# Last two layers of a gated cross-attention stack: order of scatters, of the last chunk's routing and of the first queries

## The chip, the cores and the metric

The kernel runs on one core of one Trainium2 chip. Times are microseconds on the device for one execution of the whole program, the median of several runs. The engines are TensorE (PE; its weight loads are PEld), VectorE (DVE), ScalarE (ACT), GpSimd (POOL) and SyncE (SP, which here only issues DMAs). They run side by side, each through its own list of instructions in order, and wait for each other by semaphores.

## What is computed

Four layers act on x, 2 batches of 1024 tokens of 256 features in float32. Each layer is

```
x = x + tanh(g_xattn[L]) * cross_attention_L(layernorm(x), context of 154 rows of 192)
x = x + tanh(g_ffn[L])   * ffn_L(layernorm(x))
```

The change concerns layers 2 and 3. Their attentions have 16 heads of 16. That of layer 3 normalises each whole query and each whole key to unit length, adds the unnormalised query to its output (the residual), and ends in a layer norm of its own:

```
Qp = query @ Wq + bq;  Q = l2norm(Qp);  K = l2norm(key @ Wk + bk);  V = value @ Wv + bv
out = softmax(Q K^T * SCALE) V
y = out @ Wo + bo + Qp
return (y - mean(y)) / sqrt(var(y) + 1e-5) * ln_gamma + ln_beta
```

The ffn of layer 2 is a mixture of 8 experts of width 512, each token to its top two with softmax gates, plus biases b2 by gate. That of layer 3 is a mixture of 16 experts of width 352 (top two, 320 places for each expert) plus one shared expert for all tokens.

## The kernel before

The tokens lie in 16 tiles of 128, and 4 tiles make a chunk c of 512. Phase 4 is the attention of layer 2, phase 5 its experts, phase 6 the attention of layer 3, phase 7 its experts. X holds the residual stream in SBUF, Y the normalised tokens.

The order of work in an attention of 16 heads is one list of steps, made by steps16(L) (lines 545 to 633). Every engine walks through the same list and does its own part of each step, so that a step's place in the list is its place in the queue of each engine that has a part in it, and an engine can start a step only when it is through with its parts of all steps ahead. A chunk has four groups g of four heads. The steps of a group are: "scores" (scores of the first 128 keys, four PE matmuls of 32 rows, L820, and the exponentials on ACT, L1280), "rem" (the same for the remaining 26 keys of four heads at once, L838), "av" (probabilities times values, L849 and L852, copied by ACT, L1325) and, two groups later, "norm" (transposes L861, division by the sums on DVE, L1949 and L1952). "turn back" (L868) and "tail" follow once for a chunk: tail multiplies by Wo (output, L726), and DVE adds the result, L1737 in layer 2, L1966 in layer 3.

PSUM is used as two rings of four banks, RP and RQ. An engine that takes a bank waits until the reader of the bank's previous use is through.

Preparing a chunk takes these steps in layer 3: "combine" (DVE adds the two results of layer 2's experts to X, L2359, once they have come back from DRAM), "stats" (DVE statistics L1713 and L1716, then POOL's inversion, rsqrt, L1599 and L1601), "normal" (DVE, L1722), "yT" (PE transposes L667, ACT copies L1249), "proj" (PE L779; DVE adds bq, L1921, into Y; ACT sums the squares, L1303; POOL inverts the length), "unit" (DVE scales to unit length, L1930; then POOL adds bo to Y, the residual, L1653) and "turn" (PE transposes L788, ACT copies L1313). Before the change, chunks 0 and 1 are prepared ahead of the first scores, and chunk c + 2 between the groups of chunk c (lines 592 to 599).

Behind its tail a chunk of layer 3 has "post": DVE's statistics in tail (L1969, L1972), POOL's inversion (L1661), DVE's normalisation L1977, times gamma L1982, added to X L1984. The bias ln_beta and the like is added to all of X once, by POOL (add_row, L1578), and the first use waits for it (xbias). Steps that begin with "next" belong to the routing for the experts: next stats, next normal (L1722), next yT, "next lg" (router logits, PE L1092, DVE L2381, in layer 3 softmax), "next top" (the two best of each token, one-hots, gates; in layer 2 it needs one exponential of ACT, L1415, and signals oh_made in the middle), "next pos" (PE counts places by matmuls L1100 and L1102, DVE makes slot indices in slots, L2275 to L2291; for the last chunk of layer 2 also the table of which expert each tile has, tile_table), "next scatter" (POOL issues 8 indirect DMAs for a chunk, one for each tile and choice, L1626, which write the token rows to their slots in DRAM), and in layer 2 "next G" and "next b2" (gates by expert: DVE gates_by_expert L2298 and L2300, PE transposes L1110, ACT copy L1418, PE L1118, DVE L2398). The order of POOL's work matters to the change: in it stand the inversions, the additions of bo, add_row and the scatters.

Steps that begin with "ahead" prepare keys and values of layer 3 while layer 2 still runs: "ahead keys turned" transposes the normalised keys (PE L741 and L742); DVE spreads them into even and odd heads (spread_keys, L1871), and POOL copies the last 26 keys (L1642). "ahead values" are matmuls L697 and L698 and DVE's additions (values, L1764 and L1787).

Behind the attention of layer 2 the tiled experts start: SP loads the first three W1 once tile_table is made, and the token tiles once all 32 scatters of the layer have landed (lines 2557 to 2562); PE transposes them (L1158) and multiplies (L1167, L1176). In layer 3, SP waits for all scatters likewise, and PE starts with L1190 and L1133.

The order that the diff replaces at the end of layer 2 and at the start of layer 3:

```
return o + [("av", z, 3), ("norm", z, 2), ("next yT", z - 1), ("norm", z, 3), ("next lg", z - 1),
            ("turn back", z), ("next top", z - 1), ("tail", z), ("next stats", z), ("ahead values", 0, 0),
            ("next pos", z - 1), ("next normal", z), ("next scatter", z - 1), ("next G", z - 1), ("next yT", z),
            ("ahead keys turned", 0), ("next lg", z), ("next top", z), ("ahead values", 0, 1), ("next pos", z),
            ("next scatter", z), ("next b2", z - 1), ("next G", z), ("next b2", z)]
...
o = [("combine", 0), ("stats", 0), ("combine", 1), ("normal", 0), ("yT", 0), ("stats", 1), ("proj", 0),
     ("normal", 1), ("yT", 1), ("combine", 2), ("unit", 0), ("proj", 1), ("turn", 0), ("stats", 2),
     ("unit", 1), ("turn", 1)]
```

## Time and profile before

| what | value |
|---|---|
| median of 3 runs | 1545.22 us (1532.24, 1545.22, 1550.62) |
| the profiled execution | 1543.91 us, span in the trace 1542.1 us |
| mean granted TensorE clock | 0.904 of full speed |
| busy PE, PEld, DVE, ACT, POOL | 1314.2, 812.8, 711.5, 474.8, 301.6 us |
| last matmuls ahead of the layer-2 experts, first of theirs | until 902.6 us, from 908.2 us |
| first scores of layer 3 | 1104.4 us |
| first tokens of layer 3's routed experts on PE | 1306.9 us |

All trace times count from the start of the span. Busy times overlap, since the engines run side by side; what is worth time is where PE idles or is slowed, and what it waited for there. The granted clock is 0.50 or 1.00 at any moment, so a mean between them says how much of a stretch ran at half.

### The profile page before, as it was taken

To read this page: it belongs to the slowest core of one execution; us is meant where nothing else is said; L and a number is where in the kernel's file an instruction comes from. 1 tells how busy PE (TensorE), PEld (TensorE's weight loads), DVE (VectorE), ACT (ScalarE), POOL (GpSimd) and SP (SyncE) were. 2 spreads that over 40 slices of the span, in tenths; PEclk is the share of its full clock that TensorE was granted. 3 is DMA by queue.
4 is the path that set the end of the run, shared out by engine and by line. 5 is a ranking of instruction groups with operands and counts; after the bars stand their busy time and mean duration, and the time that the engine had idled before them with its cause. 6 is when DMAs were issued, how large, how long until landed. Compare 5 with 4: busy or idle time off the path is not lost.

```text
span 1542.1 us, 18540 instructions
## 1 busy us (share of the span) xinstructions
PE 1314.2 (85%) x6487; PEld 812.8 (53%) x6513; DVE 711.5 (46%) x2010; ACT 474.8 (31%) x890; POOL 301.6 (20%) x373
## 2 busy tenths in 40 slices
PE   5999979959999856499989869994789877999997
PEld 2645444334565542354544559994544444666664
DVE  5755353386323458876563532223436464122214
ACT  1144434411222216304434113331364321222220
POOL 5200010023000010424022322222242215122220
PEclk9699989969999887769999669997799779999999
DMA  9990010010000010010000456665000022344425
GB/s 263 285 279 1 1 52 0 0 59 0 1 0 1 0 32 0 1 19 1 1 29 28 148 167 211 214 208 184 2 1 22 21 71 95 121 160 151 136 82 172
DMA packets 106201, 124.12 MB, mean 80 GB/s; under 512 B 15138, under 2 KB 90654, under 8 KB 106110
## 3 DMA queue, kind: packets, MB, share of 16 engines
q1 hardware_dynamic: 99118, 104.05, 22.9%
q0 software_dynamic: 6992, 18.88, 3.3%
q8 instruction: 54, 0.88, 0.2%
q14 instruction: 37, 0.30, 0.1%
HBM read 74.05 MB, written 48.86 MB: 80 GB/s over the span
## 4 chain that ended last, share of the span: by engine, by line
PE 74%; DVE 12%; issue 5%; POOL 4%; ACT 3%; DMA 1%; SPq 1%; DVEq 0%; POOLq 0%; ACTq 0%
PE bank L1133 9%; PE bank L726 5%; PE bank L1167 5%; PE bank L1209 4%; PE bank L1176 4%; PE bank L800 4%; PE bank L709 4%; PE bank L820 4%; PE bank L991 3%; PE bank L838 3%; PE bank L849 3%; PE bank L852 2%; PE bank L667 2%; PE bank L901 2%; POOL x_slots L1626 2%
## 5 line engine op out<-in xcount | busy, mean ns | idle before, releaser
L1280 ACT ACTIVATE scratch<-bank 128x512 f32<-128x512 f32 x240 | 126.4, 603 | 96.1 <-PE bank L827 44.2
L1133 PE MATMUL bank<-scratch 128*128 128x320 f32 (+3 forms) x480 | 154.0, 478 | 0.6 <-issue 0.6
L1599 POOL TENSOR_SCALAR rstd<-mv 128x4 f32<-128x4 f32 x36 | 10.2, 284 | 669.0 <-DVE mv L1716 644.4
L1936 DVE TENSOR_REDUCE scratch<-bank 128x2 f32<-128x308 f32 x256 | 105.7, 472 | 72.0 <-PE bank L800 69.7
L1133 PEld LDWEIGHTS bank<-scratch 128*128 128x128 f32 (+1 forms) x480 | 87.1, 185 | 61.3 <-issue 30.2
L2437 DVE TENSOR_TENSOR scratch<-scratch,bank 128x320 f32<-128x320 f32 (+3 forms) x60 | 31.4, 526 | 177.9 <-PE bank L1133 174.6
L1249 ACT ACTIVATE scratch<-bank 128x512 f32<-128x512 f32 x56 | 32.0, 599 | 222.4 <-PE bank L667 222.2
L1626 POOL DMA_INDIRECT x_slots<-scratch x64 | 66.7, 1042 | 106.3 <-DVEq L2294 88.5
L667 PE MATMUL bank<-ident,scratch 128*128 128x128 f32 x224 | 41.9, 349 | 52.9 <-DVE scratch L1722 34.5
L726 PE MATMUL bank<-weights,scratch 128*128 128x256 f32 x320 | 79.9, 409 | 6.2 <-ACT scratch L1344 2.7
L820 PE MATMUL bank<-scratch 32*128 32x512 f32 x384 | 82.2, 649 | 2.3 <-ACT scratch L1325 1.8
L800 PE MATMUL bank<-scratch 32*128 32x308 f32 x512 | 81.7, 525 | 1.3 <-DVEq L1795 1.3
L1167 PEld LDWEIGHTS bank<-scratch 128*128 128x128 f32 x624 | 77.5, 196 | 2.7 <-issue 0.8
L1167 PE MATMUL bank<-scratch 128*128 128x128 f32 x624 | 77.9, 279 | 0.4 <-issue 0.4
L1700 POOL DMA_INDIRECT y_back<-scratch x48 | 45.1, 940 | 158.2 <-ACT scratch L1474 138.9
L726 PEld LDWEIGHTS bank<-weights,scratch 128*128 128x128 f32 x320 | 64.4, 206 | 21.8 <-ACT scratch L1344 3.9
L1176 PE MATMUL bank<-scratch 128*128 x312 | 73.9, 380 | 1.3 <-ACT scratch L1430 1.3
L2420 DVE TENSOR_TENSOR scratch<-bank,weights 128x512 f32<-128x512 f32 x39 | 27.0, 692 | 103.5 <-PE bank L1167 103.5
L709 PE MATMUL bank<-scratch,weights 128*128 128x512 f32 x128 | 67.4, 680 | 5.6 <-ACT scratch L1249 5.6
L800 PEld LDWEIGHTS bank<-scratch 32*128 32x128 f32 x512 | 51.6, 207 | 34.5 <-DVE scratch L1936 11.4
L1209 PE MATMUL bank<-scratch 128*128 128x256 f32 (+3 forms) x288 | 68.9, 387 | 0.6 <-DVE scratch L2437 0.6
L667 PEld LDWEIGHTS bank<-ident,scratch 128*128 128x128 f32 x224 | 34.5, 182 | 63.7 <-issue 36.6
(372 smaller groups left out, 2300.1 us busy)
## 6 DMA issues: line engine op xcount, KB each, us to landing
scratch<-in_L_ffn_W SPq DMA_DIRECT2D x47, 512.0 KB
x_slots<-zeros SPq DMA_DIRECT2D x1, 17680.0 KB, 72.1
scratch<-y_back SPq DMA_DIRECT2D x16, 512.0 KB, 8.0
scratch<-in_L_ffn_w_gate SPq DMA_DIRECT2D x16, 352.0 KB
scratch<-in_L_ffn_w_up SPq DMA_DIRECT2D x16, 352.0 KB
x_slots<-zeros SPq DMA_DIRECT2D x1, 5200.0 KB, 89.0
scratch<-x_slots SPq DMA_DIRECT2D x39, 130.0 KB, 3.1
y_back<-zeros SPq DMA_DIRECT2D x1, 4352.0 KB, 38.7
```

Source lines behind the costliest of these rows:

```text
L667: last = pe.transpose(bk[:, i * P:(i + 1) * P], v["Y"][:, TPC * c + i, d * P:(d + 1) * P], ident[:])
L709: last = pe.matmul(bk[:], v["Wq"][:, k, m * P:(m + 1) * P], v["yT"][:, k, :], start=k == 0, stop=k == DK - 1)
L726: last = pe.matmul(bk[:, i * D:(i + 1) * D], o[:, tt * P:(tt + 1) * P], v["Wo"][:, m, :], start=m == 0, stop=m == len(rows) - 1)
L800: pe.matmul(bk[:, 0:2 * M], v["QT"][rows, c, m, t * P:(t + 1) * P], v["Kz"][rows, m, b, :, :].rearrange("p e k -> p (e k)"), start=True, s ...
L820: last = pe.matmul(bks[r][:], v["Kz"][rows, m, b, e, 0:P], v["QT"][rows, c, m, :], start=True, stop=not has_max)
L1133: last = pe.matmul(bk[0:fn, 0:n], w[s][:, k, m * P:m * P + fn], moving(k), start=k == 0, stop=k == DK - 1)
L1167: last = pe.matmul(bk[:, m * P:(m + 1) * P], v["W1"][:, i % 3, k, m * P:(m + 1) * P], v["xeT"][:, i % 2, k * P:(k + 1) * P], start=k == 0, ...
L1176: last = pe.matmul(bk[:, 0:D], v["hT"][:, i % 2, m, :], v["W2"][:, bass.ds(expert[i] * (H2 // P * D) + m * D, D)], start=m == 0, stop=m == ...
L1209: last = pe.matmul(bk[0:n, i % 2 * D:(i % 2 + 1) * D], v["hT"][0:fn, e % 2 * 3 + m, i * P:i * P + n], v["Wd"][s][0:fn, m, :], start=m == 0 ...
L1280: act.activation(v["PT"][:, n % 2, j, :], bk[:], ACT.Exp, scale=float(v["hd"]) ** -0.5).then_inc(RP.read, 1)
L1626: pool.indirect_dma_start(x2_slots if L == 2 else x3_slots, bass.IndirectOffsetOnAxis(ap=q["sidx"][:, n:n + 1], axis=0), q["Yx"][:, t, :], ...
L1936: dve.tensor_reduce(v["mx"][:, TPC * c + t, r, 2 * m:2 * m + 2], bk[:, 0:2 * M].rearrange("p (e k) -> p e k", k=M), AX.X, ALU.max)\
```

## The change

Six edits, all in the order of steps or in who does a step:

1. In both layers, "next scatter" of chunks 0 and 1 moves from group 2 to the end of group 3 of the chunk, behind the inversions of "post" and "next stats" in POOL's queue.
2. At the end of layer 2, "next pos" and "next scatter" of chunk 2, then the normalisation, come ahead of both "ahead values"; the last chunk's "next yT" and "next lg" come ahead of "ahead keys turned" and of "next G". DVE's part of G becomes a step of its own ("next gates"), ahead of the last logits for chunk 2.
3. The keys are turned through ring RP, and ACT instead of DVE spreads them; POOL's copy of the last 26 keys is a step of its own behind the last scatter.
4. Layer 3 prepares only chunk 0 ahead of the first scores. Chunks 1 to 3 are prepared between the groups of chunks 0 and 1, by two tables (first: ahead of "rem"; second: behind "av"); chunk 3's "turn" falls into chunk 2, group 0. Its combines and statistics move along.
5. POOL adds the bias row to X at chunk 1, group 1 instead of chunk 0, group 3.
6. In layer 3 the wait for that row stands in "post" of chunk 0 instead of in its tail.

```diff
             else:
-                o = [("combine", 0), ("stats", 0), ("combine", 1), ("normal", 0), ("yT", 0), ("stats", 1), ("proj", 0),
-                     ("normal", 1), ("yT", 1), ("combine", 2), ("unit", 0), ("proj", 1), ("turn", 0), ("stats", 2),
-                     ("unit", 1), ("turn", 1)]
+                o = [("combine", 0), ("stats", 0), ("normal", 0), ("yT", 0), ("combine", 1), ("proj", 0), ("stats", 1),
+                     ("unit", 0), ("normal", 1), ("turn", 0)]
+
+                first = {(0, 0): [("yT", 1), ("combine", 2)], (0, 1): [("combine", 3)], (0, 2): [("stats", 3)],
+                     (0, 3): [("normal", 3)]}
+                second = {(0, 0): [("proj", 1), ("stats", 2)], (0, 1): [("unit", 1), ("normal", 2)], (0, 2): [("turn", 1), ("yT", 2)],
+                      (0, 3): [("proj", 2)], (1, 0): [("unit", 2), ("yT", 3)], (1, 1): [("turn", 2)], (1, 2): [("proj", 3)],
+                      (1, 3): [("unit", 3)], (2, 0): [("turn", 3)]}
...
-                ahead = c + 2 < NC
+                ahead = L < 3 and c + 2 < NC
...
-                    if L == 3 and c == 0:
-                        o += {0: [("normal", 2)], 1: [("combine", 3)], 2: [], 3: []}[g]
+                    if L == 3:
+                        o += first.get((c, g), [])
...
-                            o += {0: [("next yT", c - 2)], 1: [("next lg", c - 2)], 2: [("next pos", c - 2), ("next scatter", c - 2)],
+                            o += {0: [("next yT", c - 2)], 1: [("next lg", c - 2)], 2: [("next pos", c - 2)],
                                   3: [("next b2", c - 2)]}[g]
                     if L == 3 and c > 1:
-                        o += {0: [("next normal", c - 2)], 1: [("next lg", c - 2)], 2: [("next pos", c - 2), ("next scatter", c - 2)],
+                        o += {0: [("next normal", c - 2)], 1: [("next lg", c - 2)], 2: [("next pos", c - 2)],
                               3: []}[g]
...
                         o.append(("av", *divmod(n - 1, 4)))
+                    if L == 3:
+                        o += second.get((c, g), [])
...
-                    if L == 3 and c == 0:
-                        o += {0: [], 1: [("stats", 3)], 2: [("normal", 3)], 3: []}[g]
...
-                            o += {0: [], 1: [("next top", c - 2)], 2: [("next G", c - 2)], 3: []}[g]
+                            o += {0: [], 1: [("next top", c - 2)], 2: [("next gates", c - 2), ("next G", c - 2)], 3: [("next scatter", c - 2)]}[g]
                     if L == 3:
                         if c and g == 3:
                             o += [("post", c - 1), ("next stats", c - 1)]
                         if c > 1:
-                            o += {0: [("next yT", c - 2)], 1: [("next top", c - 2)], 2: [("next res", c - 2)], 3: []}[g]
+                            o += {0: [("next yT", c - 2)], 1: [("next top", c - 2)], 2: [("next res", c - 2)], 3: [("next scatter", c - 2)]}[g]
...
-                            ("turn back", z), ("next top", z - 1), ("tail", z), ("next stats", z), ("ahead values", 0, 0),
-                            ("next pos", z - 1), ("next normal", z), ("next scatter", z - 1), ("next G", z - 1), ("next yT", z),
-                            ("ahead keys turned", 0), ("next lg", z), ("next top", z), ("ahead values", 0, 1), ("next pos", z),
-                            ("next scatter", z), ("next b2", z - 1), ("next G", z), ("next b2", z)]
+                            ("turn back", z), ("next top", z - 1), ("tail", z), ("next stats", z), ("next pos", z - 1),
+                            ("next scatter", z - 1), ("next normal", z), ("ahead values", 0, 0), ("ahead values", 0, 1),
+                            ("next yT", z), ("next gates", z - 1), ("next lg", z), ("ahead keys turned", 0), ("next G", z - 1),
+                            ("next top", z), ("next pos", z), ("next scatter", z), ("ahead last keys", 0), ("next b2", z - 1),
+                            ("next gates", z), ("next G", z), ("next b2", z)]
...
-                        bk = RQ.take(pe, p, "k", m)
+                        bk = RP.take(pe, p, "k", m)
...
+                    if what == "ahead keys turned":
+
+                        for m in range(MT):
+                            bk = RP.get(act, 6, "k", m)
+                            a = bk[:, 0:B * M].rearrange("p (b k) -> p b k", k=M)
+                            for e in range(2):
+                                st.did(act.activation(ph[6]["Kz"][:, m, :, e, :], a, ACT.Copy, scale=odd[:, e:e + 1]))
+                            st.wait()
+                            act.sem_inc(RP.read, 1)
+                            act.sem_inc(kz16_made, 1)
...
-                    elif what == "scores" and L and (c, i[0]) == (0, 3 if L == 3 else 0):
+                    elif what == "scores" and L and (c, i[0]) == ((1, 1) if L == 3 else (0, 0)):
                         add_row((v["gb"] if L == 3 else v["gbo"])[:], gbo_made, L, p)
...
-                        if L and c == 0:
+                        if L in (1, 2) and c == 0:
                             dve.wait_ge(xbias, XB[p])
...
                     elif what == "post":
+                        if c == 0:
+                            dve.wait_ge(xbias, XB[p])
                         dve.wait_ge(post_z, c + 1)
```

## Rows read from the trace of the kernel before

**Rows 1.** Windows by stage: busy time of each engine, then PEclk, DMA share, GB/s

```profile
core 0: us, PE busy (x) PEld busy (x) DVE busy (x) ACT busy (x) POOL busy (x), PEclk, DMA share, GB/s
910.00:1059.00 149.00, 147.46 (x1010) 138.96 (x1010) 40.00 (x145) 52.85 (x115) 36.28 (x38) 0.98 0.64 194
1059.00:1309.00 250.00, 189.66 (x934) 106.61 (x933) 124.23 (x415) 86.48 (x176) 78.13 (x73) 0.85 0.16 52
```

**Rows 2.** Timeline of PE, end of layer 2: start, us, line, op, [idle before <- releaser]

```profile
874.72 1.01 PE L1110 MATMUL bank<-ident,scratch 128*8 128x128 f32 x4 [4.85 <-DVE scratch L2300]
...
879.74 3.58 PE L1092 MATMUL bank<-weights,scratch 128*128 128x8 f32 x16
...
910.28 2.05 PE L1167 MATMUL bank<-scratch 128*128 128x128 f32 x8 [0.38 <-issue]
```

**Rows 3.** Timelines of DVE and, in the last row, of POOL there

```profile
884.52 0.19 DVE L2381 TENSOR_TENSOR scratch<-bank,weights 128x32 f32<-128x32 f32 x1 [3.69 <-PE bank L1092]
...
888.69 0.42 DVE L1764 TENSOR_TENSOR scratch<-bank,weights 128x256 f32<-128x256 f32 x1
...
891.25 0.17 DVE L2291 CAST scratch<-scratch 128x8 uint32<-128x8 f32 x1
...
900.66 0.96 POOL L1626 DMA_INDIRECT x_slots<-scratch  x1 [0.30 <-issue]
```

**Rows 4.** Timeline of PE, start of the last attention

```profile
1077.43 1.94 PE L667 MATMUL bank<-ident,scratch 128*128 128x128 f32 x8 [18.22 <-issue]
1080.06 6.28 PE L779 MATMUL bank<-weights,scratch 128*128 128x256 f32 x16 [0.69 <-ACT scratch L1249]
...
1090.86 6.00 PE L779 MATMUL bank<-weights,scratch 128*128 128x256 f32 x16 [0.69 <-ACT scratch L1249]
...
1102.51 1.97 PE L788 MATMUL bank<-ident,scratch 128*128 128x128 f32 x8 [4.78 <-DVE scratch L1930]
1104.41 2.15 PE L820 MATMUL bank<-scratch 32*128 32x512 f32 x8
...
1107.89 1.04 PE L667 MATMUL bank<-ident,scratch 128*128 128x128 f32 x8
...
1113.77 3.72 PE L779 MATMUL bank<-weights,scratch 128*128 128x256 f32 x16
```

**Rows 5.** Timelines of POOL, then of DVE, in the last attention

```profile
1073.80 1.99 POOL L1601 TENSOR_TENSOR rstd<-rstd,nhalf 128x4 f32<-128x4 f32 x1
...
1079.45 1.04 POOL L1601 TENSOR_TENSOR rstd<-rstd,nhalf 128x4 f32<-128x4 f32 x1
...
1103.06 2.35 POOL L1653 TENSOR_TENSOR scratch<-scratch,weights 128x1024 f32<-128x1024 f32 x1 [0.18 <-POOL rstd L1601]
...
1101.32 1.14 DVE L1930 TENSOR_SCALAR scratch<-scratch 128x256 f32<-128x256 f32 x4 [2.00 <-POOLq L1649]
1102.97 3.56 DVE L1722 TENSOR_SCALAR scratch<-X,mv,rstd 128x256 f32<-128x256 f32 x4 [0.51 <-POOLq L1570]
...
1273.24 1.37 DVE L1722 TENSOR_SCALAR scratch<-X,mv,rstd 128x256 f32<-128x256 f32 x4
```

**Rows 6.** Timeline of PE behind the projection of chunk 2

```profile
1121.20 1.13 PE L838 MATMUL bank<-scratch 128*128 128x512 f32 x2 [2.06 <-ACT scratch L1280]
```

**Rows 7.** DVE's post step in chunk 1; waits 1062:1310 (total, times, longest); PE's transposes

```profile
1162.75 1.38 DVE L1977 TENSOR_SCALAR scratch<-scratch,mv,rstd 128x256 f32<-128x256 f32 x4 [0.93 <-POOLq L1661]
...
DVE scratch L1977 <- POOLq L1661: 8.1, 3, 4.2
...
1171.53 1.09 PE L667 MATMUL bank<-ident,scratch 128*128 128x128 f32 x8 [1.93 <-DVE scratch L1722]
...
1206.98 1.97 PE L667 MATMUL bank<-ident,scratch 128*128 128x128 f32 x8 [6.45 <-DVE scratch L1722]
...
1247.80 1.97 PE L667 MATMUL bank<-ident,scratch 128*128 128x128 f32 x8 [7.38 <-DVE scratch L1722]
```

**Rows 8.** Windows from a chunk's y transposes to the end of the next output

```profile
1171.50:1189.60 18.10, 18.07 (x119) 10.50 (x119) 8.22 (x47) 8.73 (x17) 3.02 (x3) 1.00 0.04 16
1207.00:1231.70 24.70, 24.51 (x120) 13.90 (x120) 8.20 (x46) 8.95 (x17) 3.27 (x4) 0.70 0.03 12
```

8 lines of the change are left out of this document (3 added, 5 removed).

## The prediction

> **What bounds the kernel now.** I read the busy times by stage first. The stretch from 1059 to 1309 us, the last attention with the shared half of the last experts, is the loosest: TensorE (PE) is busy 189.7 of 250 us and its mean granted clock is 0.85 [rows 1]. The same view of 910 to 1059, the layer-2 experts, has PE busy 147.5 of 149, so nothing can be won there; the change touches only what lies around it. Next comes PE's own order of instructions, and in it each row that begins with idle time: those are the places where another engine is last. Last come the waits of DVE and POOL, to see which link of the chain ended each gap. PE is the bound while it is fed. It is starved at the end of layer 2, where the last scatter of tokens is late [rows 2, 3], at the start of the last attention [rows 4], and before the transposes of a normalised chunk [rows 7]. A starved place can cost twice: the idle time, and the work behind it at half clock.
>
> **Part 1: end of layer 2.** Now PE waits 4.85 us for DVE ahead of G (L1110), because DVE does values(0) and the slots ahead of the normalisation; then come the transposes of y, the turned keys and, from 879.7, the last chunk's logits (16 matmuls, 3.58 us at half clock) [rows 2]. DVE's own chain from these logits to slot indices runs from 884.5 to 891.4, 6.9 us, of which values(1), from 888.69 to the slots at about 890.5, are 1.8 with their hand-overs [rows 3]. The eighth scatter is issued until 901.6, and the first tile's matmuls start 8.7 us after that (910.28) [rows 2, 3].
> The new order: values(0) (1.8) leave DVE's queue ahead of the normalisation, so the transposes of y can start at about 873.1 (G's place less 1.6). PE does both values meanwhile: 16 matmuls of 256 columns, like the 3.72 us of the projection at full clock [rows 4]. Then at full clock 1.0 of transposes, 1.2 for the copies of ScalarE (ACT), 1.9 of logits: they are in DVE at 877.3 instead of 884.5. DVE's chain is now 5.3 (6.9 less values, plus hand-over), and up to 0.9 more, because ACT now spreads the keys, four activations, ahead of the one exponential that DVE waits for in the middle. Indices at 883.5, hand-over 0.2, eight issues of 0.96 with 0.30 between [rows 3] end at 893.7: 7.9 us earlier, and 8.9 if the exponential isn't late. At half clock the logits take 3.58 and the turned keys behind them some 2.5, the exponential is 2.2 us late for DVE, and the same sum gives 3.2. I take 5.5, the middle: PE no longer idles at 870, but it does only short work there, and the clock was half behind such work. The POOL copy of the last keys goes behind the scatter and is first read in the next attention, 150 us of experts away [rows 1]. The scatters of chunks 0 and 1 of this layer move behind one inversion of 1.3 us: nothing. The first expert weights are requested right behind the table of tiles, which moves forward too. **-5.5** (-3.2 to -8.9).
>
> **Part 2: start of the last attention.** DVE's second combine leaves the side of POOL's first inversion, whose power step took 1.99 instead of 1.04 us [rows 5], and the normalisation no longer stands behind it: the first transposes come 1.9 us earlier, at 1075.5 [rows 4]. From there PE does the transposes of y(0) (1.94), waits 0.7 for copies, projects (6.28, half clock); then comes the chain of bias, squares, inversion, scaling. For chunk 1 that chain is seen: projection's end 1096.86, turn at 1102.51, 5.65 us [rows 4]. So the turn of chunk 0 begins at 1090.2, takes 2.0 and 0.7 for the copy, and scores(0,0) start at 1093.0 instead of 1104.4: -11.4. What left the front is done between the groups: transposes 1.04, projection 3.72, turn another 1.04 at full clock [rows 4], +5.8. A projection between groups also holds the exponentials on ACT behind its squares; PE waited 2.06 us for that behind the projection of chunk 2 [rows 6], and chunk 3's does the same. In the new order chunks 1 and 2 have it, while chunk 3's projection is followed by the output matmuls, which cover it: two stalls against two; I add 0.75, because the first falls where nothing else is queued. -11.4+5.8+0.75 = **-4.85** by the end of chunk 0's output. Bounds: +1 with the moved work at half clock (it then costs 5.8 more), -8 if the stalls go.
>
> **Part 3: the last queries meet the post-norm.** In chunk 1, group 3, the step "unit 3" now stands right ahead of "post 0". Now DVE is free at 1161.82 and waits 0.93 for POOL's inversion [rows 7]. After: DVE scales the queries (1.14, L1930), only then POOL may add bo to the residual (2.35, L1653), and the inversion (about 0.3 and 1.04) is queued behind that on POOL [rows 5]. With three hand-overs of 0.1 that is 1161.82+1.14+2.35+1.35+0.3 = 1166.96 for the post step's start against 1162.75: **+4.2**. Behind it stand the post step, the statistics, the normalisation, and PE's transposes, which already waited 1.93 [rows 7]; so PE's idle becomes 6.1 us. Behind a gap of 6.45 at the same place one chunk later the stretch up to the next output took 24.7 us at mean clock 0.70, against 18.1 at 1.00 behind the gap of 1.93 [rows 7, 8]. The 120 and 119 matmuls are the same work, so I charge **+6.5** for it here; the lower bound is 0, if the clock holds. The bias row that POOL adds to X moves to chunk 1, group 1, where POOL has nothing due for two groups, and its wait moves to the post step: nothing; if POOL were held by it past the inversion, the price would be this part's again.
>
> **Part 4: scatters at a chunk's end.** In chunks 2 and 3 POOL's eight scatters (10.1 us) stand ahead of the post-norm's inversion, and DVE waits: of 8.1 us in three waits 0.9 belong to chunk 1, 4.2 and 3.0 to these [rows 7]. Behind the inversions they hold nobody up; DVE's own residual step and norm take as long as the inversion, so nothing is next: **-4.1** and **-2.9**. PE's gaps shrink from 6.45 to 2.3 and from 7.38 to 4.5 [rows 7]. Gaps of 1.93 and 2.06 had full clock behind them, so the half-clock loss of chunk 2 goes: **-6.5**. A gap of 4.78 had half clock behind it (the turn at 1102.51 took 1.97) [rows 4], so chunk 3 keeps its loss: 0, at best -2.5.
> The scatters now start together with DVE's normalisation, for which PE waits. The one such case in the trace, chunk 3's normalisation at 1273.24 with a scatter issued beside it, took 1.37 for its four instructions [rows 5]: nothing. A POOL tensor operation beside the same four made them 3.56, which is 2.2 more [rows 5]; twice that is the upper end, +4.4.
> The Trainium skill (GPSIMD Engine Reference, section Key points) says that GpSimd shares its SBUF interfaces with VectorE and contends with it in a two-port mode or with two SBUF inputs. By it alone a scatter would count like the tensor operation, and the sum would be 4.4 us higher; the row of the scatter speaks against that.
>
> **Sum.** -5.5-4.85+4.2+6.5-4.1-6.5-2.9 = -13.15. The profiled execution took 1543.91 (span 1542.1 and 1.8 around it): 1530.8. The median of the runs shown is 1.3 above that execution, so 1532. Those three runs lie within 1532 to 1551, and 1% is about what a measurement can tell from no change.
>
> **Rivals.**
> A, the clock holds behind the new gap of part 3: 1532-6.5 = 1525.5. For: the gap is 0.35 shorter than the one that lost it, and dense work (two remainder groups) stands right ahead of it. Against: the gaps of 4.78, 6.45 and 7.38 all had half clock behind them [rows 4, 7]. 0.20.
> B, the clock falls in chunk 2 too, behind the shorter gap: 1538.5. For: the work behind it is the same that did not bring the clock back for over half of 24.7 us [rows 8]. Against: it stayed full behind 1.93 at this very place. 0.15.
> C, the earlier indices gain nothing in layer 2 (the exponential behind the keys, G and b2 still to do, weights late): 1537.5. For: PE has two rounds of G and b2 left behind the slots, some 10 us. Against: the scatter and its landing take 19 from the same point, and none of the others was last before. 0.10.
> D, a scatter beside the normalisation holds it like a POOL tensor operation: 1536.4. Against: the row of 1.37. 0.07.
> E, on the other side: one late post-norm (part 3) puts PE to half clock, and until the last output it does not come back, so that the two shorter gaps find it low. A chunk of 29 us of PE work, stretched like the first stretch here (24.7/18.1) throughout, costs 10.6 instead of 6.5, and so does the next, in place of part 4's gain of 6.5: 1532+4.1+10.6+6.5 = 1553. It decides once the clock stays low for more than the one stretch of 24.7 us. Against: the mean of 0.70 says that it came back within that stretch. 0.04.
> F, the gaps move but are filled by other waits, so that it cancels: about 1545. 0.06.
> The forecast itself, 1527 to 1537: 0.38.
>
> **Numbers.** Faster by over 1% means below 1529.8: A nearly whole, and the forecast's own lower third and more (part 1 at its -8.9, a share of measurement spread): 0.41. Slower by over 1%: E, 0.04. The rest within 1%: 0.55. The range from 1520 (A with part 1's best end and a little more) to 1546 leaves out E and the tails.
>
> **What would show it.** Right: scores(0,0) some 11 us earlier after the first combine; a gap of about 6 us on PE ahead of the y(0) transposes, ended by DVE L1722, with half clock behind it; DVE's waits for the post inversion of about 4, 0 and 0 us; gaps of about 2.3 and 4.5 in chunks 2 and 3; last layer-2 scatter to first tile still 8.7 us. Wrong: the gap in chunk 1 below 3 us (then POOL's order was misread), a normalisation of over 2 us beside a scatter, or a stretch from the layer-2 experts' end to the routed experts that is not about 8 us shorter.

## The result, and the profile of the changed kernel

The changed kernel took 1532.6 us (seven runs, 1528.15 to 1533.95) against 1545.22 (seven runs, 1532.24 to 1550.62): ratio 0.9938, 95% interval 0.9909 to 0.9967. The forecast of 1532 fits, and the direction with it; the time saved is below 1%. Two later series of the same kernel gave 0.9905 (0.9867 to 0.9943) and 0.9978 (0.9951 to 1.0004), so about 9 us is a better figure for the gain than the 12.6 of the first medians. The profiled execution took 1533.95 (span 1532.2).

The windows by stage (the columns are those of [rows 1]). The first row covers the same 250 us of the span as the last row there, so it starts later in the work: it holds the last attention, the shared half of the last experts and some 11 us more of the routed ones. The second row is the layer-2 experts, which now start at 897.4.

```profile
1059.00:1309.00 250.00, 204.28 (x962) 115.14 (x962) 124.04 (x418) 87.94 (x179) 76.37 (x72) 0.82 0.14 48
897.40:1047.50 150.10, 148.21 (x1014) 138.70 (x1014) 39.99 (x145) 53.32 (x116) 36.48 (x38) 0.98 0.63 194
```

PE is busier in the 250 us (204.3 for 189.7 before), but its mean clock is lower, 0.82 for 0.85. The experts of layer 2 are as they were.

The timeline of PE has the places that [rows 2, 4, 7] showed, now with new times and gaps (start, length, line, [idle before <- releaser]; L673 is L667 of before, L794 is L788, L826 is L820, L844 is L838, L1164 is L1158, and DVE's L1738 is L1722):

```profile
869.03 1.09 PE L673 MATMUL bank<-ident,scratch 128*128 128x128 f32 x8 [0.87 <-DVE scratch L1738]
...
897.40 0.66 PE L1164 MATMUL bank<-ident,scratch 128*128 128x128 f32 x2 [5.83 <-issue]
...
1064.11 1.94 PE L673 MATMUL bank<-ident,scratch 128*128 128x128 f32 x8 [16.64 <-issue]
...
1079.02 1.97 PE L794 MATMUL bank<-ident,scratch 128*128 128x128 f32 x8 [5.65 <-DVE scratch L1944]
1081.88 2.09 PE L826 MATMUL bank<-scratch 32*128 32x512 f32 x8 [0.89 <-ACT scratch L1329]
...
1120.51 2.08 PE L844 MATMUL bank<-scratch 128*128 128x512 f32 x2 [2.06 <-ACT scratch L1286]
...
1162.51 1.97 PE L673 MATMUL bank<-ident,scratch 128*128 128x128 f32 x8 [6.01 <-DVE scratch L1738]
...
1199.93 1.97 PE L673 MATMUL bank<-ident,scratch 128*128 128x128 f32 x8 [3.84 <-DVE scratch L1738]
...
1237.44 1.97 PE L673 MATMUL bank<-ident,scratch 128*128 128x128 f32 x8 [6.74 <-DVE scratch L1738]
```

Scores(0,0) start at 1081.88 instead of 1104.41; the first combine came at 1056.76 instead of 1068.18, so 11.1 us of the 22.5 are won behind it. The gap ahead of the y(0) transposes has grown from 1.93 to 6.01 us; those of y(1) and y(2) have shrunk from 6.45 and 7.38 to 3.84 and 6.74.

The reason for the new gap stands in DVE's and POOL's timelines of chunk 1 (L1944 is "unit 3", L1669 POOL's addition of bo, L1615 and L1617 the inversion, L1993 the post step, L1977 in [rows 7]):

```profile
1148.60 1.13 DVE L1944 TENSOR_SCALAR scratch<-scratch 128x256 f32<-128x256 f32 x4
1153.75 1.38 DVE L1993 TENSOR_SCALAR scratch<-scratch,mv,rstd 128x256 f32<-128x256 f32 x4 [4.02 <-POOLq L1677]
...
1161.07 1.38 DVE L1738 TENSOR_SCALAR scratch<-X,mv,rstd 128x256 f32<-128x256 f32 x4 [0.91 <-POOLq L1586]
```

```profile
1149.81 2.35 POOL L1669 TENSOR_TENSOR scratch<-scratch,weights 128x1024 f32<-128x1024 f32 x1 [3.39 <-DVE scratch L1944]
1152.24 0.23 POOL L1615 TENSOR_SCALAR rstd<-mv 128x4 f32<-128x4 f32 x1
1152.56 1.04 POOL L1617 TENSOR_TENSOR rstd<-rstd,nhalf 128x4 f32<-128x4 f32 x1
```

That is part 3 of the prediction, link by link: scaling, addition of bo, inversion, post step. The windows behind the gaps of chunks 1 and 2 answer to [rows 8]:

```profile
1162.50:1186.10 23.60, 23.59 (x119) 13.62 (x119) 8.23 (x47) 8.95 (x17) 0.00 (x0) 0.73 0.00 1
1199.90:1223.60 23.70, 23.67 (x120) 13.69 (x120) 8.21 (x46) 8.95 (x17) 7.34 (x8) 0.73 0.13 46
```

The first ran at 1.00 before and now at 0.73, as forecast. The second should have gone from 0.70 to 1.00 and did not: the gap of 3.84 has half clock behind it, too. That is rival B, in part.

So the time fits, but these two profiles don't show it to come from where the prediction put it. Their spans differ by 9.9 us. Of these, 4.1 lie ahead of the end of layer 2's last output, 6.7 between there and the first expert tile, and 0.6 in the layer-2 experts, while the attention of layer 3, from its first combine to the y(2) transposes, is 1.1 us longer than before (180.7 for 179.6), where the prediction's parts 2 to 4 had 7.65 less; 0.5 more is lost behind it.

### The profile page after: what moved, and what is told of

The parts are those of the page before. It is cut to its first block, busy times and chain, and to the rows that moved or that the text cites. A ratio compares the mean times of both kernels' runs of the same rounds, so it can differ in the third digit from the quotient of the medians.

```text
span 1532.2 us, 18567 instructions
## 1 busy us (share of the span) xinstructions
PE 1315.4 (86%) x6513; PEld 810.8 (53%) x6513; DVE 709.6 (46%) x2006; ACT 477.1 (31%) x894; POOL 300.6 (20%) x373
## 4 chain that ended last, share of the span: by engine, by line
PE 76%; DVE 12%; issue 4%; POOL 3%; ACT 3%; DMA 1%; SPq 1%; DVEq 0%; POOLq 0%; ACTq 0%
PE bank L1139 9%; PE bank L732 5%; PE bank L1173 5%; PE bank L806 4%; PE bank L1215 4%; PE bank L1182 4%; PE bank L715 4%; PE bank L826 4%; PE bank L855 3%; PE bank L844 3%; PE bank L997 3%; PE bank L858 2%; PE bank L673 2%; PE bank L907 2%; PE bank L867 1%
## 5 line engine op out<-in xcount | busy, mean ns | idle before, releaser
L1615 POOL TENSOR_SCALAR rstd<-mv 128x4 f32<-128x4 f32 x36 | 11.2, 311 | 739.1 <-DVE mv L1732 686.1
L673 PE MATMUL bank<-ident,scratch 128*128 128x128 f32 x224 | 42.2, 351 | 51.5 <-DVE scratch L1738 34.1
L826 PE MATMUL bank<-scratch 32*128 32x512 f32 x384 | 83.6, 662 | 1.5 <-ACT scratch L1329 0.9
L1642 POOL DMA_INDIRECT x_slots<-scratch x64 | 65.4, 1022 | 29.8 <-issue 18.1
L673 PEld LDWEIGHTS bank<-ident,scratch 128*128 128x128 f32 x224 | 34.5, 183 | 62.7 <-issue 36.6
```

Source lines behind the costliest of these rows:

```text
L673: last = pe.transpose(bk[:, i * P:(i + 1) * P], v["Y"][:, TPC * c + i, d * P:(d + 1) * P], ident[:])
L826: last = pe.matmul(bks[r][:], v["Kz"][rows, m, b, e, 0:P], v["QT"][rows, c, m, :], start=True, stop=not has_max)
L1642: pool.indirect_dma_start(x2_slots if L == 2 else x3_slots, bass.IndirectOffsetOnAxis(ap=q["sidx"][:, n:n + 1], axis=0), q["Yx"][:, t, :], ...
```

## The experiments

One profile can't separate the terms, because the clock's level differs from execution to execution. So each experiment is read in two ways: by its ratio to the kernel before (measured on the same chip), and by the lengths of the stages of its profile, which repeat to 0.1 us wherever the clock does. The stages, with the starts and ends that bound them:

- R: end of the last output of layer 2 to the first expert tile
- S: first combine to the end of chunk 0's output
- T: from there to the y(0) transposes
- U: from the y(0) transposes to the end of chunk 1's output
- V: to the y(1) transposes; W: to the end of chunk 2's output; Z: to the y(2) transposes

| kernel | ratio | R | S | T | U | V | W | Z |
|---|---|---|---|---|---|---|---|---|
| before | 1 | 40.8 | 90.5 | 12.9 | 18.1 | 17.4 | 24.7 | 16.1 |
| changed | 0.9938 | 34.0 | 88.7 | 17.0 | 23.6 | 13.8 | 23.7 | 13.8 |
| e1 scatters alone | 0.9973 | 40.3 | 91.3 | 12.9 | 22.7 | 13.8 | 23.7 | 13.8 |
| e2 routing alone | 0.9974 | 36.6 | 89.2 | 12.9 | 18.0 | 17.4 | 24.7 | 16.1 |
| e3 queries alone | 0.9992 | 40.4 | 85.5 | 17.0 | 19.3 | 17.4 | 24.6 | 16.1 |
| e4 unit 3 later | 0.9965 | 37.0 | 85.0 | 12.9 | 25.1 | 13.8 | 23.8 | 13.8 |
| e5 changed again | 0.9905 | 34.2 | 85.7 | 17.0 | 19.3 | 13.8 | 22.6 | 13.8 |
| e6 without routing | 0.9938 | 39.8 | 85.0 | 17.0 | 19.3 | 13.8 | 22.6 | 13.8 |
| e7 without queries | 0.9914 | 34.2 | 90.7 | 12.9 | 18.1 | 13.8 | 22.7 | 13.8 |
| e8 without scatters | 0.9955 | 33.2 | 85.2 | 17.0 | 19.2 | 17.4 | 19.7 | 16.1 |
| e9 exponential first | 0.9958 | 34.4 | 89.0 | 17.0 | 23.6 | 13.8 | 23.7 | 13.8 |
| e10 residual earlier | 0.9948 | 37.6 | 88.5 | 17.0 | 23.6 | 12.9 | 22.5 | 12.9 |
| e11 three moves | 0.9929 | 34.8 | 85.6 | 12.9 | 25.1 | 12.9 | 21.0 | 12.9 |
| e12 changed, third | 0.9978 | 36.9 | 84.6 | 17.0 | 19.2 | 13.8 | 22.6 | 13.8 |

e1 to e4 ran on one chip, e5 to e8 on a second, e9 to e12 on a third. Half the width of the intervals is about 0.003, or 4.6 us.

**e1: the scatters alone** (of the kernel before; the lines of layer 3, those of layer 2 are alike)

```diff
-2: [("next pos", c - 2), ("next scatter", c - 2)],
+2: [("next pos", c - 2)],
...
-1: [("next top", c - 2)], 2: [("next res", c - 2)], 3: []}[g]
+1: [("next top", c - 2)], 2: [("next res", c - 2)], 3: [("next scatter", c - 2)]}[g]
```

> The kernel before with part 4 alone: the scatters of chunks 0 and 1 of both layers at the end of group 3. By the prediction's terms: DVE's waits for the post inversion in chunks 2 and 3 fall from 4.2 and 3.0 us to about 0.7 (what the profile of the changed kernel shows there), the gaps ahead of the transposes of y(1) and y(2) from 6.45 and 7.38 to about 2.5 and 4.5, and full clock behind the first of them: -13.5, so 1532. Rival (clock falls behind the shorter gap too, as in the changed kernel's profile): -7, so 1538. Rival (the whole gain of the change is this part, the rest cancels): 1532.6, the changed kernel's own time, with the clock at half in chunk 2. Rival (scatters beside the normalisation hold it): a normalisation of over 2 us in chunks 2 and 3.

Measured: 1542.44 against 1544.48, ratio 0.9973 (0.9943 to 1.0002). V and Z shrink by 3.6 and 2.3 us, and W only by 1.0: half clock behind the shorter gap, so the rival of 7 us is the nearer one, and 13.5 is out. In U, where nothing of this part stands, something else shows. PE there, behind a gap of 1.91 us:

```profile
1177.00 1.09 PE L667 MATMUL bank<-ident,scratch 128*128 128x128 f32 x8 [1.91 <-DVE scratch L1722]
1178.02 2.88 PE L820 MATMUL bank<-scratch 32*128 32x512 f32 x8
1180.83 1.11 PE L861 MATMUL bank<-ident,scratch 128*128 128x128 f32 x4
1181.74 3.43 PE L1092 MATMUL bank<-weights,scratch 128*128 128x16 f32 x16
```

The scores take 2.88, the logits 3.43 us: half clock, for some 11 us, behind the very gap that had full clock behind it in [rows 7, 8]. The prediction's argument "gaps of 1.93 and 2.06 had full clock behind them" rested on one sample of each.

**e2: the routing alone** (edits 2 and 3 of the change on the kernel before)

```diff
-("ahead values", 0, 0), ("next pos", z - 1), ("next normal", z), ("next scatter", z - 1), ("next G", z - 1), ("next yT", z),
-("ahead keys turned", 0), ("next lg", z), ("next top", z), ("ahead values", 0, 1), ("next pos", z),
+("next pos", z - 1), ("next scatter", z - 1), ("next normal", z), ("ahead values", 0, 0), ("ahead values", 0, 1),
+("next yT", z), ("next gates", z - 1), ("next lg", z), ("ahead keys turned", 0), ("next G", z - 1),
...
-bk = RQ.take(pe, p, "k", m)
+bk = RP.take(pe, p, "k", m)
```

> The kernel before with part 1 alone (end of layer 2: order, keys through RP and ACT, gates as a step of its own, last keys behind the scatter). Relative to the end of the last output of layer 2 the first expert tile should come 6.9 us earlier, as in the changed kernel's profile (record: 5.5): 1538 to 1540. The output of layer 2 itself should end at 867.3 as before, since no edit stands ahead of it: if it ends at 863.2 again, its full clock belongs to the order behind it after all, and the time is 1534. Rival (earlier indices gain nothing, weights or the copy of ACT late): 1545, same first tile.

Measured: 1540.78 against 1544.48, ratio 0.9974 (0.9949 to 0.9998). The last output of layer 2 ended at 862.9, 4.6 us earlier than before; 3.0 of them are that output itself, which took 3.72 us at full clock here and 6.72 at half clock in the kernel before. Over all 14 profiles this end lies anywhere from 858.1 to 874.3, and its mean is 867.8 with the old routing (four) and 866.5 with the new (ten): the end moves with the clock of the execution, and nothing shows it to be part of the change. R, which leaves it out, is 36.6 against 40.8. DVE waited here 4.12 us for the exponential, and 1.35 in the changed kernel; see e9.

**e3: the queries alone** (edits 4 to 6 on the kernel before)

```diff
-o = [("combine", 0), ("stats", 0), ("combine", 1), ("normal", 0), ("yT", 0), ("stats", 1), ("proj", 0),
-     ("normal", 1), ("yT", 1), ("combine", 2), ("unit", 0), ("proj", 1), ("turn", 0), ("stats", 2),
-     ("unit", 1), ("turn", 1)]
+o = [("combine", 0), ("stats", 0), ("normal", 0), ("yT", 0), ("combine", 1), ("proj", 0), ("stats", 1),
+     ("unit", 0), ("normal", 1), ("turn", 0)]
...
-elif what == "scores" and L and (c, i[0]) == (0, 3 if L == 3 else 0):
+elif what == "scores" and L and (c, i[0]) == ((1, 1) if L == 3 else (0, 0)):
```

> The kernel before with parts 2 and 3 alone (queries of chunks 1 to 3 between the groups, bias row later). Scores(0,0) 11.4 us earlier after the first combine; end of chunk 0's output 1.7 to 4.85 us earlier (profile of the changed kernel: 1.7); gap of 6.0 us ahead of the y(0) transposes and 23.6 instead of 18.1 us behind it: by the record +5.9, by the profile of the changed kernel +7.9, so 1551 to 1553. Rival (the work between the groups is covered, the new gap is free): -5 to -9, so 1536 to 1540.

Measured: 1545.7 against 1544.48, ratio 0.9992 (0.9962 to 1.0023): neither +5.9 nor -5. S is 4.9 shorter, as the prediction had it (4.85), T 4.1 longer (predicted 4.2). But U is 19.3 and not 23.6:

```profile
1171.82 1.97 PE L672 MATMUL bank<-ident,scratch 128*128 128x128 f32 x8 [6.04 <-DVE scratch L1727]
1173.72 2.26 PE L825 MATMUL bank<-scratch 32*128 32x512 f32 x8
1175.91 0.66 PE L866 MATMUL bank<-ident,scratch 128*128 128x128 f32 x4
1176.41 1.86 PE L1097 MATMUL bank<-weights,scratch 128*128 128x16 f32 x16
```

Behind 6.04 us of idle the transposes (1.97 for 1.09) and most of the scores are slow, then the logits take 1.86: the clock is back after some 4 us, which costs 1.2 in all.

**e4: unit 3 later** (of the changed kernel)

```diff
-(1, 3): [("unit", 3)], (2, 0): [("turn", 3)]}
+(2, 0): [("unit", 3)], (2, 1): [("turn", 3)]}
```

> The changed kernel with the scaling of chunk 3's queries (unit 3) moved from chunk 1, group 3 to chunk 2, group 0, and their turn to group 1. DVE's wait for the post inversion in chunk 1 falls from 4.02 to about 0.9 us, the gap ahead of the y(0) transposes from 6.01 to about 2, and full clock behind it (18.1 instead of 23.6 us): -4 and -5.5, so 1523. Then the clock may be full in chunk 2 as well or fall there behind the gap of 3.84 as now. Rival (the clock is lost in one place or the next whatever the gap): -4 alone, 1528.5. Rival (the gap costs nothing, since the chain behind it is DVE's): 1532.6. Rival (POOL's addition of bo now falls beside the normalisation of y(0), which takes 3.56 instead of 1.38): 1525 and a gap of 4.

Measured: 1540.18 against 1544.48, ratio 0.9965 (0.9938 to 0.9992). DVE's wait is 0.98 us, as expected, T is back at 12.9, and PE's gap halves. It is 2.96 rather than 2, since the turn (1.04) no longer stands in it:

```profile
1164.19 1.37 PE L673 MATMUL bank<-ident,scratch 128*128 128x128 f32 x8 [2.96 <-DVE scratch L1738]
1165.50 2.83 PE L826 MATMUL bank<-scratch 32*128 32x512 f32 x8
...
1169.16 3.43 PE L1098 MATMUL bank<-weights,scratch 128*128 128x16 f32 x16
...
1176.13 1.93 PE L858 MATMUL bank<-scratch 128*32 128x512 f32 x8
```

And yet U is 25.1 (1.33 of it the turn that came in): half clock for over 12 us behind the shorter gap. T and U together, which hold the same work in both orders, are 38.1 us here, 40.6 in the first profile of the changed kernel and 36.3 in e5. The rival "lost in one place or the next whatever the gap" is what this profile shows. The rival of the slowed normalisation is refuted: the normalisation of y(0) took 1.38 us, since POOL's addition of bo came behind it. So the cause of the new wait is settled (the scaling and POOL's addition of bo ahead of the inversion: 4.02 us for 0.98), and its clock price is not a matter of its length.

**e5: the changed kernel again** (no edit)

> The changed kernel itself once more, beside the three kernels that lack one part each. The parts alone moved the median by -2.0 (scatters), -3.7 (routing) and +1.2 us (queries with the late bias addition). If they simply add, the changed kernel is 4.5 us below the kernel before, about 1540. If the record's sum holds, and so the parts help each other, it is 12 to 13 below, as in its first seven runs: 1532. A spread of under 6 us over its runs, as there, would say that the order is steadier against the clock's level; a spread of some 15 us, like that of all the others, that seven runs had luck.

Measured: 1527.01 (six runs, 1521.78 to 1533.37) against 1540.35, ratio 0.9905 (0.9867 to 0.9943). The spread is 11.6 us, so the 5.8 of the first seven runs were luck. The profile differs from that of the first run in the clock. Window U of this kernel, then the rows of both behind the same gap of 2.06 us in chunk 0, this kernel's first:

```profile
1155.90:1175.20 19.30, 19.30 (x119) 11.34 (x119) 8.23 (x47) 8.84 (x17) 0.00 (x0) 0.91 0.00 1
```

```profile
1115.46 1.13 PE L844 MATMUL bank<-scratch 128*128 128x512 f32 x2 [2.06 <-ACT scratch L1286]
1116.51 1.07 PE L855 MATMUL bank<-scratch 128*32 128x512 f32 x8
```

```profile
1120.51 2.08 PE L844 MATMUL bank<-scratch 128*128 128x512 f32 x2 [2.06 <-ACT scratch L1286]
1122.51 1.71 PE L855 MATMUL bank<-scratch 128*32 128x512 f32 x8
```

Same program, same gap to 0.01 us, full clock ahead of it in both (the scores there took 1.14 us), and half clock behind it in one execution only. The two had parted before: the first projection took 6.63 us in the first profile and 5.69 here. The two outcomes go on: the three profiles with S of 88.5 to 89.0 have U of 23.6, the five with S of 84.6 to 85.7 and the same gap ahead of U have 19.2 or 19.3. That is 8 us between executions of one kernel, in two stages alone. It goes on into W: behind the gap of 3.84, PE here still had full clock in the transposes (1.09 for 1.97) and half clock only from the scores on:

```profile
1188.98 1.09 PE L673 MATMUL bank<-ident,scratch 128*128 128x128 f32 x8 [3.84 <-DVE scratch L1738]
1190.00 2.88 PE L826 MATMUL bank<-scratch 32*128 32x512 f32 x8
```

The four profiles that begin so (e5, e6, e7, e12) have W of 22.6 or 22.7, and their U was 18.1 to 19.3; the four at half clock from the transposes on (the first profile, e1, e4, e9) have W of 23.7 or 23.8, and their U was 22.7 to 25.1.

**e6: without the routing** (the first lines of e2's diff, and the rest of edits 2 and 3, taken back from the changed kernel)

```diff
-("next pos", z - 1), ("next scatter", z - 1), ("next normal", z), ("ahead values", 0, 0), ("ahead values", 0, 1),
+("ahead values", 0, 0), ("next pos", z - 1), ("next normal", z), ("next scatter", z - 1), ("next G", z - 1), ("next yT", z),
```

> The changed kernel with the end of layer 2 as before (parts 2, 3 and 4 left). By the record part 1 is worth 5.5 us, by the first profile of the changed kernel 6.9, by the run of it alone 3.7: so this one is 3.7 to 6.9 us slower than the changed kernel of the same call, and the first expert tile comes 8.7 us behind the last scatter as in all others. Rival (part 1 gave nothing, the clock did): the same time as the changed kernel within 2 us.

Measured: 1530.98 against 1527.01 for the changed kernel, ratio 0.9938 (0.9906 to 0.9970) against 0.9905: 4.0 us by the medians, 5 by the ratios. R is 39.8 against 34.2. Part 1 gives what it should; "nothing" is unlikely, though the two intervals overlap. The first tile's transposes start 7.8 us behind the start of the last scatter's issue in both.

**e7: without the queries** (edits 4 to 6 taken back from the changed kernel; one line of it)

```diff
-ahead = L < 3 and c + 2 < NC
+ahead = c + 2 < NC
```

> The changed kernel with the start of layer 3's attention as before (parts 1 and 4 left). By the record parts 2 and 3 cost 5.9 us together, so this one is 5.9 faster than the changed kernel of the same call; by the run of them alone 1.2 faster. Gap ahead of the y(0) transposes back at about 1.9 us with full clock behind it. Rival (preparing less ahead of the first scores is worth its 11 us, the late bias addition costs only what DVE waits): 1 to 5 us slower than the changed kernel.

Measured: 1525.93, ratio 0.9914 (0.9882 to 0.9947), the same as the changed kernel (0.9905). Stage by stage, S is 5.0 longer, T 4.1 shorter, U 1.2 shorter: the three cancel to 0.3 us. So parts 2 and 3 together are worth nothing in these two series, and neither the prediction's loss of 5.9 nor the rival's loss came.

**e8: without the scatters** (edit 1 taken back in both layers)

```diff
-2: [("next pos", c - 2)],
+2: [("next pos", c - 2), ("next scatter", c - 2)],
...
-2: [("next res", c - 2)], 3: [("next scatter", c - 2)]}[g]
+2: [("next res", c - 2)], 3: []}[g]
```

> The changed kernel with the scatters of chunks 0 and 1 back in group 2 (parts 1, 2 and 3 left). By the record part 4 is worth 13.5 us, by the profiles 7 (DVE's waits of 4.2 and 3.0 back, the clock at half in chunk 2 in either case), by the run of it alone 2.0. So it is 2 to 7 us slower than the changed kernel of the same call, with gaps of 6.5 and 7.4 us ahead of the transposes of y(1) and y(2) instead of 3.84 and 6.74.

Measured: 1536.37, ratio 0.9955 (0.9932 to 0.9977), 9.4 us above the changed kernel by the medians and 7.7 by the ratios. V and Z are back at 17.4 and 16.1, the gaps 7.41 and 9.04. W, however, is the shortest of all, behind a gap of 7.41:

```profile
1204.80:1224.50 19.70, 19.70 (x120) 11.31 (x120) 8.21 (x46) 8.84 (x17) 3.24 (x4) 0.89 0.04 15
```

With that, stages R to Z sum to only 1.5 us more than in e5, though V and Z alone are 5.9 more. The larger part of the difference between the two profiles lies ahead of R: the last output of layer 2 ended at 872.2 here and at 858.1 in e5. The scatters of layer 2 stand there, but over all profiles this end is at 866.5 with them moved (ten) and 867.8 without (four), so the 9.4 is not all the part's.

**e9: the exponential first**

```diff
-("next lg", z), ("ahead keys turned", 0), ("next G", z - 1), ("next top", z),
+("next lg", z), ("next top", z), ("ahead keys turned", 0), ("next G", z - 1),
```

> The changed kernel with the last chunk's two best (and so the exponential) ahead of the turned keys. In the changed kernel DVE waits 1.4 to 1.6 us for the exponential, which stands behind four key copies (2 x 0.92 us) and the copy of G on ACT. Expected: that wait falls under 0.3 us and the stretch from the last y transposes to the first expert tile shrinks from 28.5 to about 27.1: -1.4, too small for the median to show (interval of some 0.3%), so the stretch decides. Rival (the tiles wait for something else, the weights or the table): the wait goes and the stretch stays 28.5.

Measured: 1539.38, ratio 0.9958 (0.9932 to 0.9984); e12 had 1538.02. By the stage, R is 34.4 (34.8 in e11, which has this move too). In the eight profiles with the changed order of routing DVE waited 1.22 to 1.36 us for the exponential in four (R 33.2 to 34.2) and 4.1 to 4.5 in four (R 36.6 to 37.6). A long case, from e12, on DVE and on ACT (L1309 the key copies, L1434 G, L1431 the exponential), and then ACT in e9:

```profile
887.23 0.17 DVE L2267 TENSOR_SCALAR scratch<-scratch 128x4 f32<-128x4 f32 x1 [4.37 <-ACT scratch L1431]
```

```profile
882.51 0.93 ACT L1309 ACTIVATE scratch<-bank,odd 128x308 f32<-128x308 f32 x2 [6.14 <-PE bank L748]
885.40 0.93 ACT L1309 ACTIVATE scratch<-bank,odd 128x308 f32<-128x308 f32 x2 [1.96 <-remote]
886.51 0.59 ACT L1434 ACTIVATE scratch<-bank 8x512 f32<-8x512 f32 x1 [0.19 <-ACT scratch L1309]
887.01 0.19 ACT L1431 ACTIVATE scratch<-scratch 128x4 f32<-128x4 f32 x1
```

```profile
879.06 0.20 ACT L1431 ACTIVATE scratch<-scratch 128x4 f32<-128x4 f32 x1 [4.71 <-DVEq L2252]
881.21 0.93 ACT L1309 ACTIVATE scratch<-bank,odd 128x308 f32<-128x308 f32 x2 [1.94 <-issue]
883.38 0.93 ACT L1309 ACTIVATE scratch<-bank,odd 128x308 f32<-128x308 f32 x2 [1.25 <-remote]
```

In the four long cases ACT idles 1.96 to 3.34 us between the two pairs of key copies, in the short ones 0.35 or 0.36, for a reason that the trace doesn't name. With the exponential ahead of them DVE doesn't wait, and ACT's idle time hits nobody. Against the long case the move is worth 2 to 3 us. Against the short one (R 33.2 to 34.2) it shows nothing; in e9 DVE idled 0.74 and 0.98 us in its own chain instead, with no other engine named.

**e10: the residual earlier**

```diff
-1: [("next top", c - 2)], 2: [("next res", c - 2)], 3: [("next scatter", c - 2)]
+1: [("next top", c - 2), ("next res", c - 2)], 2: [], 3: [("next scatter", c - 2)]
```

> The changed kernel with the residual step (L2416, 1.25 us on DVE) behind the two best in group 1 instead of between the statistics and the post step in group 2. In chunks 2 and 3 POOL's first step of the post inversion took 1.17 us beside it instead of 0.23. Expected: 0.23 again, DVE's wait for the inversion still about 0.7 to 0.9, and the gaps ahead of the transposes of y(1) and y(2) 0.94 us smaller each, 3.84 to 2.9 and 6.75 to 5.8: -1.9. Rival (contention was not with the residual step): 1.17 stays and the gaps stay.

Measured: 1536.83, ratio 0.9948 (0.9912 to 0.9983). V and Z are 12.9 for 13.8. In the changed kernel the residual step (L2416), POOL's first step of the inversion beside it, and DVE's wait for the inversion in chunk 2; then the inversion's first step and PE's gap in e10:

```profile
1188.61 1.25 DVE L2416 SCALAR_TENSOR_TENSOR X<-scratch,tg,X 128x1024 f32<-128x1024 f32 x1
```

```profile
1188.78 1.17 POOL L1615 TENSOR_SCALAR rstd<-mv 128x4 f32<-128x4 f32 x1 [27.79 <-DVE mv L1986]
```

```profile
1191.16 1.38 DVE L1993 TENSOR_SCALAR scratch<-scratch,mv,rstd 128x256 f32<-128x256 f32 x4 [0.66 <-POOLq L1677]
```

```profile
1195.86 0.23 POOL L1615 TENSOR_SCALAR rstd<-mv 128x4 f32<-128x4 f32 x1 [27.77 <-DVE mv L1986]
```

```profile
1206.06 1.33 PE L673 MATMUL bank<-ident,scratch 128*128 128x128 f32 x5 [2.90 <-DVE scratch L1738]
```

As expected to 0.05 us: 0.94 for each chunk, and contention with the residual step is its cause. The Trainium skill (GPSIMD Engine Reference, section Key points) says that GpSimd shares its SBUF interfaces with VectorE and that the two contend when the VectorE instruction is in a two-port mode or has two SBUF inputs. The residual step has two SBUF inputs, and the pair 1.17 and 0.23 agrees.

**e11: three moves together** (e4, e9 and e10)

> The changed kernel with three moves together: the exponential first (-1.4), the residual earlier (-1.9), and unit 3 behind the post step of chunk 0, in chunk 2, group 0 with its turn in group 1 (-4.1 for the stretch from the output of chunk 0 to the y(0) transposes, 12.9 instead of 17.0, as in the kernel that moved it alone). Sum -7.4, so some 7 us below the changed kernel of this call if the clock behind the gap comes back as fast as it does behind the gap of 6.0 us (the next stretch then 20.3, which is 19.3 and the turn of 1.04). Rival (the clock stays at half for some 12 us behind this gap, as in the one profile of the move alone, 25.1): about 2 us below, the rest lost.

Measured: 1534.2 against 1538.02 for the changed kernel beside it, ratio 0.9929 (0.9904 to 0.9954) against 0.9978. That is 3.8 us by the medians and 7.6 by the ratios, between the two expectations. T, V and Z are 12.9 each, none shorter in any kernel, and U is 25.1 again:

```profile
1168.60:1193.80 25.20, 25.14 (x127) 14.60 (x127) 10.43 (x52) 10.04 (x19) 2.35 (x1) 0.73 0.00 1
```

Its median is the lowest of e9 to e12, and it is probably a few us better than the changed kernel; the intervals of the two ratios just touch.

**e12: the changed kernel a third time** (no edit)

> The changed kernel a third time, as the comparison for the other three of this call. Its ratio to the kernel before was 0.9938 and 0.9905; expected 0.990 to 0.994. The stretch from the first combine to the end of chunk 0's output was 88.7 us in its first profile and 85.0 to 85.6 in four others with the same order: expected 85.3 (a clock that fell once) and, behind the y(0) transposes, 19.3 rather than 23.6. If 88.7 and 23.6 come again, they belong to the order and part 2 and 3 are worse than the other profiles say.

Measured: 1538.02 (twelve runs, 1531.01 to 1548.1) against 1542.6, ratio 0.9978 (0.9951 to 1.0004), worse than expected. The stages are the expected ones, S 84.6 and U 19.2 (window at mean clock 0.91); R is in its long case. The first profile's 88.7 and 23.6 are not fixed by the order: they came in three of the ten profiles that start layer 3's attention the new way (the first, e9, e10).

## Why the prediction was right, and where only by cancellation

The terms of the sum against the stages, each as the mean over all profiles with the part less the mean over all without it (T, V and Z do not vary):

| term | forecast | measured |
|---|---|---|
| part 1, R (8 with, 4 without) | -5.5 | -4.9 |
| part 2, S (10 and 4) | -4.85 | -4.2; -5.2 without the three at 88.5 to 89.0 |
| part 3, wait for the inversion, T | +4.2 | +4.1 |
| part 3, half clock, U (8 and 4) | +6.5 | +1.7 |
| part 4, wait in chunk 2, V | -4.1 | -3.6 |
| part 4, full clock in chunk 2, W (8 and 4) | -6.5 | -0.2 |
| part 4, wait in chunk 3, Z | -2.9 | -2.3 |
| sum | -13.15 | -9.4 |

The sum of the last column agrees with the three ratios, whose mean, 0.9940, is -9.2 us. Two of its terms hang on single profiles of the kernels that lack the part: without e1's 22.7 part 3's clock term is +2.8, and without e8's 19.7 part 4's is -1.5.

The forecast of 1532 against 1532.6 is partly luck. The waits below were worked out rightly, but the two clock terms, on the table's figures, were wrong by 4.8 and 6.3 us, in opposite directions.

- **The waits were read right.** Every term that follows a chain of instructions through the queues came within 0.7 us: values out of DVE's queue, the shorter start, the scaling and the addition of bo ahead of the inversion (DVE's wait of 4.02 where "about 4" stood), the scatters behind the inversions.
- **The step that failed: "Gaps of 1.93 and 2.06 had full clock behind them, so the half-clock loss of chunk 2 goes: -6.5".** It took the clock's level behind a gap for a function of the gap's length, with one sample for each length. The runs show both levels behind the same gap: 2.06 us in the changed kernel's first and second profile, 1.9 us in the kernel before and in e1. And behind the shorter gap of 3.84, stage W took 22.6 to 23.8 us in all eight profiles, for 18.1 of a chunk at full clock, while one of 7.41 (e8) cost only 1.6 us. So W hardly changed. Nor is it the gap's length alone: the same work behind the same 3.84 us began at full clock in four profiles and at half in the other four (see e5).
- **The same step in part 3, "so I charge +6.5 for it here", was mis-sized:** half clock is there every time, but in five of eight profiles it lasts some 4 us and costs 1.2; in three it costs 5.5. That is 2.8 in the mean; it is +1.7 in the table because one profile without the part (e1) lost 4.6 there too. The two errors, -4.8 and +6.3, nearly cancelled, and only so did the sum come near. Rival B (clock lost in chunk 2) came true, and rival A (clock not lost behind the new gap) mostly.
- **Part 1** was charged "up to 0.9 more" for the exponential; DVE waits 1.3 or 4.4. R shrank by 6.4 in the four profiles with the short wait and by 3.3 in the four with the long one, so both stayed inside the range. The doubt about the whole part, rival C, is refuted: R shrank in all eight.
- **Part 4 lost 0.5 of each term** to a thing not foreseen. With the scatters gone, the inversion became the link behind the statistics, and its first step ran beside the residual step at 1.17 us. "DVE's own residual step and norm take as long as the inversion, so nothing is next" missed that the inversion is slowed beside the residual step (e10). PE's gaps were also forecast too small, 2.3 and 4.5 for the 3.84 and 6.74 measured. They shrank by only 2.6 and 0.6; the rest of V and Z came off ahead of them, where PE had idled 0.68 and 1.59 us for ACT.
- **Rival D** is refuted: in chunk 2 the normalisation, with a scatter issued 0.8 us behind its start, took 1.38. It is POOL that can pay: the scatter issued beside the normalisation at 1273.24 of [rows 5] took 1.78 us, where the first scatters of chunks 2 and 3 took 1.10. **Rival E** is too: the clock came back in every profile. **Rival F** is wrong as a whole but true of parts 2 and 3, which cancel each other (e7).
- **One of the signs of being wrong** was "a stretch from the layer-2 experts' end to the routed experts that is not about 8 us shorter". On PE it took 247.7 us before. In the five profiles with the changed kernel's order there it took 248.7 (the first), 250.1 (e9), 240.2 (e5), 240.1 (e12) and 239.1 (e6). So the sign of error came in two, the forecast saving in three, and the mean is 4.1 shorter.
- The size of the first difference, 12.6, owes some 3 us to the kernel before having run slower in those seven runs than later (1545.2 against 1540.4, 1542.6 and 1544.5). The changed kernel's own three medians are 1532.6, 1527.0 and 1538.0.

What stays open: what decides between the two clock levels behind one and the same gap, and what ACT waits for in the long case of R. Whether the move of unit 3 always leads to the long half clock was seen only twice (e4, e11). No kernel was tried in which POOL's addition of bo goes to another engine.

## What to carry to other kernels

Follow waits through the queues link by link: those terms came out within a microsecond. Do not spend a clock gain on them from one sample; give half clock behind a gap both prices that the trace shows (here 1.2 and 5.5 us) and a chance, since two executions of one program differ. And where a median moves by less than half a per cent, compare stage lengths of many profiles: where the clock is the same they repeat to 0.1 us, while the total spreads by 15.

## What the runs showed of the hardware that was not expected

- The granted clock behind the same idle time of PE, in the same program, was 0.5 in one execution and 1.0 in another (2.06 us of idle: the remainder matmuls took 2.08 and 1.13 us). With what followed in two stages, executions of one kernel differed by 8 us; whole executions of one kernel spread by up to 22 us here (e3).
- A POOL operation on 128x4 elements took 1.17 us beside a DVE operation with two SBUF inputs of 128x1024, and 0.23 alone. The DVE operation itself took 1.25 beside it and 1.28 in e10, where POOL was idle: only POOL paid. It began 0.17 us after the DVE operation and ended 0.09 us after it.
- ACT idled 1.96 to 3.34 us between two pairs of identical copies whose inputs were ready, in four of the eight profiles with this order, and 0.35 or 0.36 in the others.
